# Expert weights split inside the attention loop, and token blocks of two halves taken in turn

## The chip, the cores and the metric

The kernel runs on one core of one Trainium2 chip. The metric is the device time of the whole launch in microseconds (us); lower is better. Engines are TensorE (PE in the profile), VectorE (DVE), ScalarE (ACT), GpSimd (POOL) and SyncE (SP). SyncE computes nothing here: its queue only issues transfers.

## The reference, cut to what matters

N is 4096 rows, D is 512 columns, there are 8 experts and each row takes 2 of them.

```python
q = layernorm(x) @ Wq.T + bq;  k = key @ Wk.T + bk;  v = value @ Wv.T + bv
s = (q @ k.T) / 64 * adj
s = where(abs(s) < 1e-5, -1e9, s)
x = x + softmax(s) @ v @ Wm.T + bm
z = layernorm(x)
gate = softmax(z @ Wg + bg)                     # 8 experts, the 2 largest kept and normalised
x = x + sum over the 2 experts of gate_e * (z @ We[e].T + be[e])
```

## The kernel before, in words

**Precision.** Every large matrix is held as two float16 halves, a high one and a low one (the rest after the high one is taken off), and a product is three matrix multiplications (high by high, high by low, low by high). ScalarE makes the high half, VectorE the low one.

**First stage.** Weights are folded, keys and values laid in two SBUF regions (`key_region`, `val_region`), queries sent to DRAM (`q_scratch`). The change doesn't touch it.

**Attention loop.** 32 tiles of 128 rows (T is 32), each in 8 chunks of 512 columns (C is 8). In iteration t TensorE computes the scores of tile t (`scores`) and the product of tile t-1's probabilities with the values (`times_values`), which runs two chunks late: chunks 6 and 7 of tile t-2 fall into the start of iteration t. One iteration on TensorE is in order: scores 0, scores 1, values 6 of t-2, scores 2, values 7 of t-2, scores 3, values 0 of t-1, scores 4, and so on. `times_values` of chunk 0 waits for `x1_done`, because the one PSUM bank of the output (`o_bank`) must have been read by `residual` of tile t-2 on VectorE (L1009). VectorE's iteration (`attend`, L1142) is in order: `low_half` of the probabilities of t-1 (L989), `times_adj` (L967), `mask` (L974, L977), after chunk 2 `residual` and the layer norm of tile t-2, later its routing (`route_top2`, `route_gates`, `route_slots`), at the end `softmax_bias` (L983, L985). ScalarE's (L757): two exponentials for each chunk of t-1 (L745, L750), each `absolute` of t (L737), the high half of the normalised row (`split_rows`) and one small exponential of the gates. ScalarE's first exponential waits for `softmax_bias`. SyncE's queue issues the adjacency, the transposes of the probabilities (`turn_probs`, L474), the transposed rows (`turn_rows`, L480), and at the end of the iteration the next query tile (L503).

**Routing.** GpSimd scatters each row, with its number and gate, into a DRAM table `slots[h]`, one for each half of the 4096 rows (`scatter_row`, L630); each expert has a region in it. After a half, `tables` (L1091) makes on VectorE the list of that half's 39 blocks of 128 slots with their experts, and `pad_regions` (L505) fills the ends of the regions from SyncE's queue: 8 transfers, each behind a load of a register from SBUF. `tables` uses some words of the buffer `q1_words`.

**The last tile.** Tile 31 has no scores beside it. The weights' buffers lie over the loop's, so here the code is written out: ScalarE's exponentials alternate with `expert_hi` and VectorE's `low_half` with `expert_lo`, which split the 8 experts' float32 weights into halves, 16 pieces of 128x1024, of which 8 come here and 8 in the first steps of the next stage. The weights come by 8 transfers of 1 MB into two buffers and the biases by one of 2 MB. `scatter_rows` of GpSimd waits for its transfers before it goes on to `inverse_deviation` of the next tile.

**Expert stage.** 78 blocks (39 of each half, half 0 first). For each: SyncE loads 128 rows (`load_block`, a ring of 8 buffers), TensorE transposes them (`turn_block`, two blocks ahead, L1430), ScalarE and VectorE make the halves (`block_hi`, `block_lo`), TensorE multiplies by the expert (`multiply_block`, L1280 to L1282, 12 multiplications), VectorE adds the bias (L1240), ScalarE multiplies by the gate (L822), GpSimd adds the rows in DRAM by an indirect transfer (L662). An add that starts another expert waits until those before it have landed. The first 23 blocks (EARLY) are written out with the remaining pieces of weights and the routing of tile 31 between them (its scatters after adds 10 and 13, its tables after block 9); the pads of half 1 are issued by SyncE before its block 23.

## Time and profile before

| | |
|---|---|
| median of 3 runs | 1904.72 us (1899.04 to 1904.8) |
| the profiled execution | 1899.79 us |
| its span, first to last instruction | 1898.1 us |
| TensorE busy | 1817.8 us, 96% of the span |
| VectorE, ScalarE, GpSimd busy | 62%, 38%, 13% |
| mean granted TensorE clock | 0.981 of full speed |

The profiled execution lies 1.7 us above its own span and 4.9 us below the median. A busy share is a mean over stages; the last sixth of the span looks otherwise than the loop, and the rows below are chosen by stage.

### The profile page before, as it was taken

How to read it: one execution, taken by the hardware profiler on the slowest of the kernel's cores; microseconds unless marked ns; L12 is line 12 of the kernel's file. 1: busy time of each engine (PE TensorE's matmuls, PEld its weight loads, DVE VectorE, ACT ScalarE, POOL GpSimd, SP SyncE). 2: the span in 40 equal slices, each digit the busy share in tenths (PEclk: the TensorE clock that was granted, in tenths of full speed). 3: DMA queues.
4: the chain of work that ended last, by engine and by line, in shares of the span. 5: the costliest groups of instructions: out<-in, count | busy, mean ns of one | idle time of the engine just before them, and what ended most of it. 6: DMA issues, size and time to landing. Idle time of an engine off the chain costs nothing.

```text
span 1898.1 us, 32739 instructions
## 1 busy us (share of the span) xinstructions
PE 1817.8 (96%) x8730; PEld 851.0 (45%) x8731; DVE 1176.2 (62%) x3056; ACT 730.1 (38%) x1381; POOL 239.4 (13%) x277
## 2 busy tenths in 40 slices
PE   8999999999999999999999999999999996789994
PEld 4544444444444444444444444444444443345552
DVE  2788766666666666666666666666666664634542
ACT  1444444443333344433333344433333442433341
POOL 1000000100000000000000000000000010444454
PEclk9999999999999999999999999999999998899997
DMA  5355455555555555555556555555555558788785
GB/s 200 111 177 188 172 136 124 140 142 137 139 138 133 133 133 145 137 142 134 139 128 176 135 135 144 134 145 133 138 133 136 134 137 244 180 194 165 162 161 78
DMA packets 410860, 279.67 MB, mean 147 GB/s; under 512 B 316737, under 2 KB 316737, under 8 KB 410690
## 3 DMA queue, kind: packets, MB, share of 16 engines
q1 hardware_dynamic: 390914, 234.55, 47.8%
q0 software_dynamic: 16736, 38.35, 10.2%
q10 hardware_dynamic: 3168, 6.29, 1.0%
q8 instruction: 16, 0.26, 0.1%
q14 instruction: 26, 0.21, 0.0%
HBM read 144.29 MB, written 59.33 MB: 107 GB/s over the span
## 4 chain that ended last, share of the span: by engine, by line
PE 75%; DVE 8%; DMA 7%; issue 5%; SPq 2%; ACT 2%; DVEq 0%; POOLq 0%; POOL 0%; ACTq 0%
PE ps L1280 16%; PE ps L1282 16%; PE ps L1281 16%; PE ps L1380 8%; PE ps L1381 8%; PE ps L1382 8%; DMA work<-q_scratch 4%; DVE work L967 2%; PE ps L1289 2%; PE ps L1430 1%; ACT work L737 1%; DMA work<-in_WeT 1%; DMA work<-work 1%; PE ps L1327 1%; DVE work L974 1%
## 5 line engine op out<-in xcount | busy, mean ns | idle before, releaser
L1280 PE MATMUL ps<-key_region,work 128*128 128x512 f16 (+1 forms) x1336 | 509.9, 382 | 9.8 <-DMA work<-q_scratch 7.0
L1281 PE MATMUL ps<-key_region,work 128*128 128x512 f16 (+1 forms) x1336 | 509.4, 381 | 0.0
L1282 PE MATMUL ps<-key_region,work 128*128 128x512 f16 (+1 forms) x1336 | 509.2, 381 | 0.0
L1380 PE MATMUL ps<-val_region,work 128*128 128x512 f16 x1024 | 389.6, 380 | 16.3 <-DMA work<-work 11.4
L737 ACT ACTIVATE work<-work 128x512 f32<-128x512 f32 x256 | 161.3, 630 | 597.2 <-DVE work L967 597.1
L1382 PE MATMUL ps<-val_region,work 128*128 128x512 f16 x1024 | 389.6, 380 | 0.0
L1381 PE MATMUL ps<-val_region,work 128*128 128x512 f16 x1024 | 389.5, 380 | 0.0
L967 DVE SCALAR_TENSOR_TENSOR work<-ps,r_cur,work 128x512 f32<-128x512 f32 x256 | 191.8, 749 | 179.0 <-PE ps L1282 163.3
L989 DVE TENSOR_TENSOR work<-work 128x512 f16<-128x512 f32 x256 | 176.4, 689 | 84.0 <-ACT work L750 83.1
L977 DVE CUSTOM_DVE_ANT_0 work<-work 128x512 f32<-128x512 f32 x256 | 177.3, 693 | 51.2 <-DVE work L974 51.0
L1280 PEld LDWEIGHTS ps<-key_region,work 128*128 128x128 f16 x1336 | 131.2, 98 | 172.9 <-issue 28.8
L745 ACT ACTIVATE work<-work,exp_bias 128x512 f32<-128x512 f32 x256 | 181.4, 708 | 65.6 <-DVE exp_bias L985 61.5
L1282 PEld LDWEIGHTS ps<-key_region,work 128*128 128x128 f16 x1336 | 131.4, 98 | 158.8 <-issue 3.4
L1281 PEld LDWEIGHTS ps<-key_region,work 128*128 128x128 f16 x1336 | 131.3, 98 | 148.0 <-issue 3.0
L750 ACT ACTIVATE work<-work,exp_bias 128x512 f16<-128x512 f32 x256 | 180.7, 706 | 0.0
L974 DVE TENSOR_SCALAR work<-work 128x512 f32<-128x512 f32 x256 | 109.2, 426 | 113.2 <-ACT work L737 109.2
L1380 PEld LDWEIGHTS ps<-val_region,work 128*128 128x128 f16 x1024 | 100.2, 98 | 131.8 <-DMA work<-work 12.0
L1382 PEld LDWEIGHTS ps<-val_region,work 128*128 128x128 f16 x1024 | 100.4, 98 | 122.0 <-issue 1.9
L1381 PEld LDWEIGHTS ps<-val_region,work 128*128 128x128 f16 x1024 | 100.4, 98 | 114.0 <-issue 1.5
L662 POOL DMA_INDIRECT out<-val_region,tok_ids x78 | 123.9, 1588 | 152.7 <-DMA out<-val_region,tok_ids 66.6
L627 POOL COPY work<-gate 128x1 f32<-128x1 f32 x64 | 14.6, 228 | 856.9 <-DVE slots_u L1089 776.6
L822 ACT ACTIVATE val_region<-work,tok_gates 128x512 f32<-128x512 f32 x78 | 56.3, 722 | 160.6 <-DVE work L1240 138.8
(149 smaller groups left out, 1542.9 us busy)
## 6 DMA issues: line engine op xcount, KB each, us to landing
work<-in_adj SPq DMA_DIRECT2D x256, 256.0 KB, 2.8
work<-slots SPq DMA_DIRECT2D x40, 257.0 KB
val_region<-slots SPq DMA_DIRECT2D x38, 257.0 KB
work<-in_valueT SPq DMA_DIRECT2D x8, 1024.0 KB, 6.8
work<-in_x SPq DMA_DIRECT2D x8, 1024.0 KB, 5.0
work<-in_keyT SPq DMA_DIRECT2D x8, 1024.0 KB, 5.4
q_scratch<-work SPq DMA_DIRECT2D x8, 1024.0 KB, 5.0
work<-q_scratch SPq DMA_DIRECT2D x32, 256.0 KB, 3.0
```

Of the source, the lines that this page charges most:

```text
L737: nc.scalar.activation(w[:, c * CW:(c + 1) * CW], s_adj[:, c % 2, :], ACT.Abs).then_inc(abs_done, 1)
L745: nc.scalar.activation(prob[:, c % 2, :], w[:, c * CW:(c + 1) * CW], ACT.Exp, bias=exp_bias[:, :], scale=1.0 / SS, accum_out=sum_part[:, c ...
L750: nc.scalar.activation(p_split[:, c, 0:CW], w[:, c * CW:(c + 1) * CW], ACT.Exp, bias=exp_bias[:, :], scale=1.0 / SS).then_inc(p_hi, 1)
L967: nc.vector.scalar_tensor_tensor(s_adj[:, c % 2, :], s_bank(c), r_cur[:, :], adj_in[:, c % ADJ, :], ALU.add, ALU.mult).then_inc(s_read, 1)
L977: nc.vector.tensor_tensor_reduce(out=masked, in0=s_adj[:, c % 2, :], in1=masked, scale=1.0, scalar=-3.0e38, op0=ALU.add, op1=ALU.max, accu ...
L989: nc.vector.tensor_tensor(p_split[:, c, CW:2 * CW], prob[:, c % 2, :], p_split[:, c, 0:CW], ALU.subtract).then_inc(p_lo, 1)
L1280: nc.tensor.matmul(bank, st[0], mv[0], start=(k == 0), stop=False)
L1281: nc.tensor.matmul(bank, st[0], mv[1], start=False, stop=False)
L1282: last = nc.tensor.matmul(bank, st[1], mv[0], start=False, stop=(k == n - 1))
L1380: nc.tensor.matmul(o_bank, st[0], mv[0], start=first, stop=False)
L1381: nc.tensor.matmul(o_bank, st[0], mv[1], start=False, stop=False)
L1382: last = nc.tensor.matmul(o_bank, st[1], mv[0], start=False, stop=final)
```

## The change

- Iterations 2 to 17 of the loop each take one half expert (256 of its 512 inputs). It is cut in 4 pieces of 128x256: ScalarE's queue loads a piece (`load_piece`), ScalarE makes the high half (`piece_high`), VectorE the low one (`piece_low`), and ScalarE's queue stores both to a DRAM tensor `we_halves` (`store_piece`). The buffers are in `q1_words`; so VectorE waits for all stores before `tables(0)`.
- In the last tile nothing is split. ScalarE's queue loads the finished halves, one expert at a time: experts 0 to 2 around the last exponentials, 3 to 7 in steps 0 to 4 of the expert stage, each with its own row of biases. SyncE tells TensorE by `we_ready` that an expert is there. The values product of tile 31 goes to another bank (`o_last`), so it doesn't wait for `residual` of tile 30.
- GpSimd no longer waits at the end of `scatter_rows`; it makes the deviations of tiles 30 and 31 before it scatters their rows, and tile 31's rows have a buffer of their own (`row_last`). `ranks` and `route_slots` of tile 30 move behind block 0 and 1, tile 31's routing comes at blocks 4 and 6, its scatters after adds 6 and 8.
- Blocks: 15 of half 0 (LEAD), then 48 in which half 0 and half 1 alternate, then 15 of half 1. The ring of row buffers has 16 places. The pads of half 1 are issued by ScalarE after block 9, and SyncE waits for them before its block 15.

The core of the diff:

```diff
-    EARLY = 23
-    LATE = 7
+    LEAD = 15
+    AHEAD = 2
+    TOKS = 16
...
 scalar
+            def load_piece(i, q):
+                nc.scalar.dma_start(we_stage, weT_parts[i, :, q // 2, q % 2, :]).then_inc(piece_loaded, 16)
+            def store_piece(i, q):
+                act.wait_ge(piece_lo, i * PIECES + q + 1)
+                settle()
+                nc.scalar.dma_start(we_dram[i, :, :, q * WP:(q + 1) * WP], we_halves).then_inc(piece_stored, 16)
+            def piece_high(i, q):
+                act.wait_ge(piece_loaded, i * (PIECES * 16) + (q + 1) * 16)
+                if not (is0(i) and q == 0):
+                    act.wait_ge(piece_stored, i * (PIECES * 16) + q * 16)
+                nc.scalar.activation(we_halves[:, 0, :], we_stage, ACT.Copy, scale=WS).then_inc(piece_hi, 1)
+            def attend(t, routes, splits=False):
+                if splits:
+                    load_piece(t - 2, 0)
                 for c in range(4):
                     exponent(t - 1, c)
                 absolute(t, 0)
+                if splits:
+                    piece_high(t - 2, 0)
                 exponent(t - 1, 4)
                 absolute(t, 1)
                 for c in range(5, C):
                     exponent(t - 1, c)
+                if splits:
+                    store_piece(t - 2, 0)
+                    load_piece(t - 2, 1)
...
                 absolute(t, 7)
+                if splits:
+                    piece_high(t - 2, 3)
+                    store_piece(t - 2, 3)
...
+            act.wait_ge(piece_stored, 16 * PIECES * 2 * E)
+            act.wait_ge(s_mm, T * C)
+            load_expert(0)
             for c in range(C):
                 exponent(T - 1, c)
-                if c >= 4:
-                    expert_hi(c - 4)
-                if c == 6:
-                    split_rows(T - 2)
+                if c == 3:
+                    load_expert(1)
+            act.wait_ge(p_hi, T * C)
+            load_bias(0)
+            load_bias(1)
+            split_rows(T - 2)
+            load_expert(2)
+            load_bias(2)
...
+                if st.first + 3 < E:
+                    load_expert(st.first + 3)
+                    load_bias(st.first + 3)
+                if st.first == 9:
+                    act.wait_ge(tables_done, 2)
+                    for e in range(E):
+                        at = act.value_load(pad_at[0:1, 1, e:e + 1], min_val=0, max_val=(DUMMY - 1) * P)
+                        nc.scalar.dma_start(slots[1][bass.ds(at, P), :], pad_row[:, :]).then_inc(padded[1], 16)
 vector
+            def piece_low(i, q):
+                dve.wait_ge(piece_hi, i * PIECES + q + 1)
+                nc.vector.scalar_tensor_tensor(we_halves[:, 1, :], we_stage, WS, we_halves[:, 0, :],
+                                               ALU.mult, ALU.subtract).then_inc(piece_lo, 1)
             def attend(t, h=None):
...
                 mask(t, 0)
+                if splits:
+                    piece_low(t - 2, 0)
                 times_adj(t, 1)
...
                 softmax_bias(t)
+                if splits:
+                    piece_low(t - 2, 3)
...
+            dve.wait_ge(piece_stored, 16 * PIECES * 2 * E)
             tables(0)
 sync
-            sp.dma_start(we_in[0], weT_v[0]).then_inc(we_loaded[0], 16)
-            for c in range(4):
+            for c in range(5):
                 turn_probs(T - 1, c)
+                if c == 3:
+                    residual_io(T - 2, 1)
             turn_rows(T - 2)
+            for c in range(5, C):
+                turn_probs(T - 1, c)
...
+            for e in range(2, E):
+                expert_ready(e)
+            sp.wait_ge(slotted, 32 * T)
+            sp.wait_ge(padded[1], 16 * E)
+            for st in turn_steps(0):
+                load_block(st)
 tensor
-                if c == 0 and not is0(t):
+                if c == 0 and isl(t, T):
+                    pe.wait_ge(s_read, T * C)
+                elif c == 0 and not is0(t):
                     pe.wait_ge(x1_done, t)
+                bank = o_last if isl(t, T) else o_bank
```

## Rows read from the trace of the kernel before

**Rows 1.** The page's first part: busy time, share and instructions by engine.
```profile
PE 1817.8 (96%) x8730; PEld 851.0 (45%) x8731; DVE 1176.2 (62%) x3056; ACT 730.1 (38%) x1381; POOL 239.4 (13%) x277
```
**Rows 2.** Windows, from:to, length, busy by engine, PE clock, DMA share, GB/s.
```profile
706.00:748.00 42.00, 41.77 (x203) 18.91 (x202) 26.95 (x75) 16.52 (x34) 3.04 (x5) 1.00 0.56 137
...
1560.60:1600.50 39.90, 26.65 (x116) 11.65 (x115) 19.84 (x50) 14.91 (x24) 3.23 (x5) 0.83 0.93 256
1600.50:1688.40 87.90, 73.55 (x347) 36.38 (x345) 48.91 (x141) 32.60 (x51) 36.43 (x26) 0.90 0.70 170
...
1697.40:1870.70 173.30, 173.30 (x904) 93.15 (x904) 83.58 (x221) 67.10 (x111) 80.16 (x52) 0.99 0.84 164
1870.70:1898.10 27.40, 0.03 (x1) 0.00 (x0) 0.69 (x1) 0.72 (x1) 9.25 (x6) 0.57 0.45 58
```
**Rows 3.** Timeline of TensorE after 1560 us: what began after its long gaps.
```profile
1562.78 0.38 PE L1380 MATMUL ps<-val_region,work 128*128 128x512 f16 x1 [1.82 <-DVE work L1009]
...
1576.27 0.39 PE L1380 MATMUL ps<-val_region,work 128*128 128x512 f16 x1 [2.97 <-DMA work<-work]
...
1589.05 0.61 PE L1380 MATMUL ps<-val_region,work 128*128 128x512 f16 x1 [8.46 <-DMA work<-work]
...
1617.08 1.09 PE L1430 MATMUL ps<-ident,val_region 128*128 128x128 f32 x4 [5.33 <-DVE work L1232]
...
1658.99 0.68 PE L1430 MATMUL ps<-ident,val_region 128*128 128x128 f32 x4 [2.83 <-DVE work L1232]
...
1697.40 1.11 PE L1430 MATMUL ps<-ident,val_region 128*128 128x128 f32 x4 [9.05 <-DMA val_region<-slots]
```
**Rows 4.** Timeline of TensorE, expert stage: transposes of two blocks, 14 blocks apart.
```profile
1711.03 0.60 PE L1430 MATMUL ps<-ident,work 128*128 128x128 f32 x4
...
1753.40 0.60 PE L1430 MATMUL ps<-ident,work 128*128 128x128 f32 x4
```
**Rows 5.** Timeline of one loop iteration: VectorE, ScalarE and TensorE around two hand-overs.
```profile
682.05 0.75 DVE L1009 SCALAR_TENSOR_TENSOR work<-ps,inv_sum,work 128x512 f32<-128x512 f32 x1
...
683.74 0.38 PE L1380 MATMUL ps<-val_region,work 128*128 128x512 f16 x1
...
680.15 0.63 ACT L737 ACTIVATE work<-work 128x512 f32<-128x512 f32 x1 [0.18 <-DVE work L967]
...
708.54 0.15 DVE L985 TENSOR_SCALAR exp_bias<-row_max 128x1 f32<-128x1 f32 x1
...
708.82 0.72 ACT L745 ACTIVATE work<-work,exp_bias 128x512 f32<-128x512 f32 x1 [1.88 <-DVE exp_bias L985]
```
**Rows 6.** Timeline of iteration 18, the one after tables(0): VectorE and TensorE.
```profile
980.82 0.75 DVE L1009 SCALAR_TENSOR_TENSOR work<-ps,inv_sum,work 128x512 f32<-128x512 f32 x1
...
981.71 0.38 PE L1380 MATMUL ps<-val_region,work 128*128 128x512 f16 x1 [3.04 <-DVE work L1009]
```
**Rows 7.** Timeline of ScalarE and VectorE: an issue of its queue, and pieces by length.
```profile
1617.57 0.38 ACTq L796 DMA_DIRECT2D work<-in_WeT  x1
1618.19 1.04 ACT L798 ACTIVATE key_region<-work 128x1024 f16<-128x1024 f32 x1
...
1621.13 0.68 DVE L1240 SCALAR_TENSOR_TENSOR work<-ps,work 128x512 f32<-128x512 f32 x1
1623.55 1.22 DVE L1197 SCALAR_TENSOR_TENSOR key_region<-work,key_region 128x1024 f16<-128x1024 f32 x1 [1.74 <-ACT key_region L798]
```
**Rows 8.** DMA issues: out<-in, queue, count, KB each, median us from issue to landing.
```profile
out<-work SPq DMA_DIRECT2D x32, 256.0 KB, 3.1
```
**Rows 9.** Timeline of SyncE's queue: pads of half 0, transposes of tile 31, pads of half 1.
```profile
1006.21 8.35 SPq L511 DMA_DIRECT2D slots<-pad_row  x8
...
1577.58 11.18 SPq L474 DMA_TRANSPOSE work<-work  x3
...
1681.56 11.26 SPq L511 DMA_DIRECT2D slots<-pad_row  x8
```
**Rows 10.** Timeline of VectorE: layer norm of tile 31, waiting for GpSimd.
```profile
1610.99 0.55 DVE L1032 TENSOR_SCALAR work<-work,moments,rstd 128x512 f32<-128x512 f32 x1 [6.20 <-POOL rstd L618]
```

More of the change, by code:

```diff
@@ L336, in graph_attention_moe_kernel @@
         padded = [sem(f"padded{h}") for h in range(HALVES)]
-        tok_loaded = [sem(f"tok_loaded{b}") for b in range(RING)]
+        tok_loaded = [sem(f"tok_loaded{b}") for b in range(TOKS)]
         tok_meta = sem("tok_meta")
@@ L371, in has, with ahead, lead_steps, turn_steps @@
             def has(self, back):
[L372 to L398 removed]
+                return self.later or self.first >= back
+            def ahead(self):
+                return Step(self.first + AHEAD, self.turn)
+        def lead_steps():
+            return [Step(s) for s in range(LEAD)]
+        def turn_steps(j, later=False):
+            return [Step(LEAD + i, j, later) for i in range(TURN)]
+        def tail_steps():
+            return [Step(s) for s in range(SEQ - LEAD, SEQ)]
+        TURNS = (SEQ - 2 * LEAD) // TURN
         block = ctx.enter_context(nc.Block())
@@ L626, in scatter_row @@
                 settle()
-                nc.gpsimd.tensor_copy(row_gate, gate[:, i:i + 1]).then_inc(gate_put, 1)
+                row = row_last if isl(t, T) else row_buf
+                nc.gpsimd.tensor_copy(row[:, D + 1:D + 2], gate[:, i:i + 1]).then_inc(gate_put, 1)
                 pool.wait_ge(gate_put, t * 2 + i + 1)
@@ L1168, in attend @@
                     route_low(t - 2, h)
+                if splits:
+                    piece_low(t - 2, 1)
                 mask(t, 4)
@@ L1172, in attend @@
                 times_adj(t, 6)
+                if splits:
+                    piece_low(t - 2, 2)
                 mask(t, 6)
@@ L1246, in _ @@
             route_stats(T - 1)
-            dve.wait_ge(be_loaded, 16)
             dve.wait_ge(tables_done, 1)
-            for i, st in enumerate(early_steps()):
-                if SPLIT_EARLY + i < 2 * E:
-                    expert_lo(SPLIT_EARLY + i)
-                block_lo(ahead(st))
-                if i == 0:
+            for st in lead:
+                block_lo(st.ahead())
+                if st.first == 0:
                     route_rows(T - 1)
                 block_bias(st)
-                if i == 0:
+                if st.first == 0:
                     route_low(T - 1, 1)
-                if i == 6:
+                if st.first == 4:
                     route_top2(T - 1)
                     route_gates(T - 1)
-                if i == 9:
+                if st.first == 1:
+                    route_slots(T - 2)
+                if st.first == 6:
                     route_slots(T - 1)
@@ L1264, in _ @@
             dve.wait_ge(tables_done, 2)
-            with dve.Fori(0, MIDDLE) as j:
-                for st in middle_steps(j):
-                    block_lo(ahead(st))
+            with dve.Fori(0, TURNS) as j:
+                for st in turn_steps(j):
+                    block_lo(st.ahead())
                     block_bias(st)
-            for st in end_steps():
+            for st in tail_steps():
                 if st.first + AHEAD < SEQ:
-                    block_lo(ahead(st))
+                    block_lo(st.ahead())
                 block_bias(st)
```

320 lines of the change are left out of this document (154 added, 166 removed).

## The prediction

> **What bounds the kernel now.** I read the page first: TensorE is busy for 96% of the span [rows 1], so time is won only where it is idle, or where its clock is low. The windows show where that is. An iteration of the loop keeps it busy 41.77 of 42 us [rows 2]; up to 1560.6 us little is to be had. After that there are three stretches. From 1560.6 to 1600.5 us (the values product of tile 31) it is busy 26.65 of 39.9 us at a mean clock of 0.83. From 1600.5 to 1688.4 us (the first blocks) 73.55 of 87.9 us at 0.90. From 1697.4 to 1870.7 us it never stops. The timeline names the gaps: two of 2.97 and 8.46 us behind transposes of probabilities, 5.33 us behind VectorE, 2.83 us behind VectorE while it makes the tables, 9.05 us behind a load of rows [rows 3]. What these stretches would take without gaps: the values product is 96 multiplications at 0.216 us (starts in a row on the timeline), 20.7 us, so 39.9 - 20.7 = 19.2 us are lost there. A block takes (1753.40 - 1711.03) / 14 = 3.03 us [rows 4], 78 of them 236.1 us; the stage takes 1870.7 - 1600.5 = 270.2 us, so 34.1 us are lost. The last 27.4 us [rows 2] are adds in DRAM after TensorE's end. Their number, and the half they belong to, stay as they are: 0.
>
> **What the change costs in the loop.** Each of iterations 2 to 17 gets 4 pieces on ScalarE and VectorE and 8 issues on ScalarE's queue. By busy time that is nothing: VectorE has 15 us to spare and ScalarE 25 in 42 [rows 2]. The question is where they stand in the chain, and two places matter.
>
> First, the iteration's end. ScalarE's first exponential now starts 0.28 us after `softmax_bias` starts [rows 5]. In the new order `piece_low` 3 comes behind `softmax_bias`, ScalarE waits for it, then issues the store, goes round the loop, issues the load of the next piece 0, and only then takes the exponential. A VectorE piece of 1024 columns takes 1.22 us and one of 512 0.68 us [rows 7]; the same line gives 0.41 us for 256. An issue takes 0.38 us [rows 7]. While a long ACTIVATE runs it is hidden (the ACTIVATE that follows this row starts as the earlier one ends), but here nothing runs. Sum: 0.41 + 2 x 0.38 + 0.3 for the semaphore, the registers and the branch (my choice between 0 and 0.8) = 1.5 us late.
>
> Second, inside it. `piece_low` 0 stands between `mask` 0 and `times_adj` 1, and the exponentials 5 to 7 hang on that: 0.4 us. A store and a load are issued between the last exponential and `absolute` 2 (680.15 us, [rows 5]): 0.76 us of issue, of which the running exponential hides all but some 0.2 us (between 0 and 0.5). `piece_low` 2 falls in a wait of VectorE for `absolute` 6, and pieces 1 and 3 of ScalarE in its waits: 0.
>
> So `residual` of the tile before comes 1.5 + 0.4 + 0.2 = 2.1 us later, and TensorE's values chunk 0 waits for it. What cover is there? `residual` starts at 682.05 us and TensorE takes that chunk at 683.74 us without a gap [rows 5]. In iteration 18 it did have to wait, and began 981.71 - 980.82 = 0.89 us after `residual` started [rows 6]. The cover is 683.74 - 682.05 - 0.89 = 0.8 us. TensorE would stand 2.1 - 0.8 = 1.3 us in each of the 15 iterations that have a piece 3 before them, and nothing gives it back, for everything behind it is paced by TensorE again. 15 x 1.3 = 19.5 us. Bounds: without the 0.3 and 0.2 it is 0.8 us, 12 us in all; with 0.8 and 0.5 it is 2.1 us, 31 us in all.
>
> Then `tables(0)`: VectorE now waits until the last store has landed. It is issued about 0.8 us after the bias and takes some 3.1 us to land, as a store to DRAM does [rows 8], where before `route_slots` ended 1 us after the bias. About 2.9 us go onto a gap that exists already, 3.04 us [rows 6], with no cover left. Loop: 19.5 + 2.9 = 22.4 us lost.
>
> The Trainium skill ("DMA: Bandwidth & Descriptors", section "Anatomy of one DMA — SWDGE (gpsimd) path") puts the dispatch of a transfer by the sequencer at about 50 ns. The row of this trace has 0.38 us for ScalarE's queue, so the row decides. By the page's figure two issues would cost 0.1 us in place of 0.76, the stall would be 0.65 us and the loop would lose about 13 us.
>
> **What it wins in the last tile.** The wait of 1.82 us for `residual` goes (another bank). Chunks 0 to 3 have their transposes early, chunk 4 follows. Chunk 5 now stands behind `turn_rows` of tile 30, whose row needs GpSimd, then ScalarE behind its last exponential: about 1570. With 1.25 MB of weights in flight its transpose lands at about 1578 us (before, three of them took 11.18 us to issue beside the weights and biases, [rows 9]), 5 us after TensorE wants it; the slower clock behind that costs some 3 us, the transposes of two blocks 1 us. Loss 9 in place of 19.2: 10 us won (6 to 14).
>
> **What it wins in the blocks.** Gone: the splitting of eight pieces beside the blocks, the wait of VectorE for GpSimd (6.20 us, [rows 10]) that led to TensorE's 5.33 us, and SyncE's pads ahead of the load that gave 9.05 us [rows 3]. Kept or new: the tables 2.8 us [rows 3]; the gates of tile 31 wait for tile 30's scatters, 1.5 us; block 6 is loaded behind `turn_rows`, beside 6 MB of weights, 1 us. The pads: SyncE's queue took 8.35 and 11.26 us for eight [rows 9]. ScalarE now does that with block 12 waiting behind it. Take 9.3 us. The cover is what the tables show: 5.5 us of VectorE cost TensorE 2.83 us [rows 3], so 2.7 us; 6.6 us are left. Then the pads must land before SyncE may load block 15: 2.5 us more. Slow clock 1.7 us. Sum: 2.8 + 1.5 + 1 + 6.6 + 2.5 + 1.7 = 16.1 in place of 34.1: 18 us won (9 to 23). Alternating the halves is 0: as many blocks, loads and starts of experts as before.
>
> **Sum.** -10 - 18 + 22.4 = -5.6 us. Against the profiled execution, 1899.79 us, that is 1894 us; against the median, which lies 4.9 us higher, 1899 us. I say 1898.
>
> **Rivals.**
> - *ScalarE's issues are hidden in the loop.* The queue might run ahead of the engine at the end too. For: it does so behind an ACTIVATE [rows 7]. Against: the store waits for VectorE, so it can't be early. Stall 0.65 us, loop 13 us: 1889 us. The skill's dispatch figure points the same way.
> - *The pads cost little.* If ScalarE's eight issues take 0.6 us each, or the ring of 16 rows covers them, 9 us less is lost: 1889 us.
> - *The loop loses more.* Late by 2.7 us in place of 2.1 (register work of the queue at the top): 15 x 1.9 + 2.9 = 31 us: 1908 us.
> - *The weights are in the way.* Five experts, 6.3 MB, are asked for in 15 us, while the stretch at 1560 us moved 256 GB/s at a share of 0.93 [rows 2]; that is 25 us of all the transfers. Rows, pads and scatters come late, and the tail wins only 14 us: 1912 us.
> - *The other side: TensorE's clock falls at each stall of the loop.* After 2.83 us of idle it ran low for a while (clock 0.90 in that stretch), after 3.04 us at iteration 18 it didn't. A fall costs 1.7 us a time (12 multiplications at twice 0.216). From 4 of 15 iterations on the gain is gone; with all 15, +25 us: 1923 us.
>
> **How the numbers follow.** The sum as forecast 0.36; issues hidden 0.17; cheap pads 0.12; loop loses more 0.10; weights in the way 0.15; clock 0.10. A measurement tells about 0.3%, 5.7 us, from no change. Faster: 0.17 + 0.12 + 0.16 of the forecast's own spread (1892 to 1905 us) = 0.45. Same: 0.20 + 0.10 = 0.30. Slower 0.25. The range leaves out the clock case and a little below: 1884 to 1917 us.
>
> **What would show it.** In the profile after: iterations 3 to 17 of 43.4 us in place of 42.1, each with a gap of 1.3 us on TensorE behind VectorE's `residual`, those from 19 on unchanged; a gap of about 6 us at iteration 18; the values product of tile 31 in about 30 us with one gap at chunk 5; a gap of about 6 us behind ScalarE's pads and then one behind the load of block 15. It is wrong if the loop's gap is absent (then faster by 20 us or more), or if the first 15 blocks lose over 25 us.

## The result, and the profile after

The changed kernel takes 1917.6 us (median of 5 runs, 1911.48 to 1919.96), the kernel before 1904.72 us beside it (5 runs, 1899.04 to 1907.65): a ratio of 1.007, 95% interval 1.0051 to 1.0088. It is slower, where I had forecast 1898 us. The span of the profiled execution grew from 1898.1 to 1913.1 us, by 15.0 us.

The page first: engines, the share of the chain by engine, and one group of instructions (busy time, mean ns of one, idle time just before them).

```profile
PE 1816.2 (95%) x8730; PEld 847.7 (44%) x8731; DVE 1181.4 (62%) x3104; ACT 736.7 (39%) x1429; POOL 244.5 (13%) x277
...
PE 55%; DVE 13%; DMA 12%; issue 9%; ACT 7%; SPq 2%; ACTq 1%; POOLq 1%; DVEq 1%; POOL 0%
...
L1444 PE MATMUL ps<-val_region,work 128*128 128x512 f16 x1024 | 389.9, 381 | 31.9 <-DVE work L1067 25.9
```

TensorE does the same work as before [rows 1]. The third row is the answer in small: the first multiplication of a values chunk waits 31.9 us in all, 25.9 of them for line 1067, which is `residual`. The windows put the rest in place; they are an iteration of the loop, the values product of tile 31, the first blocks, the blocks without gaps, and the adds behind the last product.

```profile
653.23:696.93 43.70, 42.02 (x202) 18.84 (x203) 28.42 (x79) 17.85 (x38) 3.28 (x5) 1.00 0.66 156
1588.67:1620.80 32.13, 25.19 (x113) 11.01 (x114) 10.26 (x34) 6.27 (x14) 2.22 (x3) 0.89 0.97 212
1620.80:1705.00 84.20, 64.33 (x323) 33.16 (x322) 38.87 (x132) 23.70 (x39) 31.97 (x26) 0.92 0.93 252
1705.00:1883.10 178.10, 177.76 (x932) 95.33 (x930) 87.15 (x230) 70.16 (x116) 85.42 (x55) 1.00 0.81 153
1883.10:1913.10 30.00, 0.00 (x0) 0.00 (x0) 0.69 (x1) 0.72 (x1) 9.32 (x6) 0.55 0.49 63
```

Beside [rows 2] that gives a ledger. Up to the values product of tile 31: 1588.67 against 1560.6 us, +28.1. The values product: 32.1 against 39.9, -7.8. All blocks: 262.3 against 270.1, -7.8. The adds behind them: 30.0 against 27.4, +2.6. Sum +15.1. (The loop began 1.5 us earlier in this execution, so it lost 29.6 us itself. The window of [rows 2] begins 0.36 us ahead of the gap in front of chunk 0, mine at that gap; from the same point the loop lost 29.2 us and the values product won 7.4.)

TensorE's timeline, what began after its gaps: the first row is one of the 15 iterations, the second iteration 18, then tile 31 and the blocks.

```profile
653.23 0.38 PE L1444 MATMUL ps<-val_region,work 128*128 128x512 f16 x1 [1.26 <-DVE work L1067]
...
1006.48 0.59 PE L1444 MATMUL ps<-val_region,work 128*128 128x512 f16 x1 [5.15 <-DVE work L1067]
...
1590.54 0.39 PE L1444 MATMUL ps<-val_region,work 128*128 128x512 f16 x1 [1.87 <-DMA work<-work]
...
1597.20 0.61 PE L1444 MATMUL ps<-val_region,work 128*128 128x512 f16 x1 [3.90 <-DMA work<-work]
...
1610.54 0.39 PE L1444 MATMUL ps<-val_region,work 128*128 128x512 f16 x1 [0.18 <-DMA work<-work]
...
1638.60 1.12 PE L1494 MATMUL ps<-ident,val_region 128*128 128x128 f32 x4 [4.58 <-DMA val_region<-slots]
...
1648.57 0.18 PE L1461 MATMUL ps<-picked,tri_half 128*128 128x8 f16 x1 [1.27 <-DVE picked L1139]
...
1678.14 1.09 PE L1494 MATMUL ps<-ident,val_region 128*128 128x128 f32 x4 [8.81 <-DVE work L1293]
...
1685.48 0.66 PE L1494 MATMUL ps<-ident,val_region 128*128 128x128 f32 x4 [2.61 <-DMA val_region<-slots]
```

And the hand-over at the end of an iteration, which answers to [rows 5]: the bias, the split of the last piece, the store, the load, the first exponential, and `residual`.

```profile
678.01 0.15 DVE L1043 TENSOR_SCALAR exp_bias<-row_max 128x1 f32<-128x1 f32 x1
678.11 0.43 DVE L1206 SCALAR_TENSOR_TENSOR work<-work 128x256 f16<-128x256 f32 x1
...
678.77 0.57 ACTq L775 DMA_DIRECT2D we_halves<-work  x1
...
679.83 0.35 ACTq L769 DMA_DIRECT2D work<-in_WeT  x1
...
680.31 0.72 ACT L751 ACTIVATE work<-work,exp_bias 128x512 f32<-128x512 f32 x1 [3.58 <-issue]
...
696.04 0.75 DVE L1067 SCALAR_TENSOR_TENSOR work<-ps,inv_sum,work 128x512 f32<-128x512 f32 x1
```

The reader is to see a chain in which each row waits for the one above. The exponential starts 2.30 us behind the bias, where it was 0.28 [rows 5]. `residual` comes 696.04 - 678.01 = 18.03 us behind the bias. In the kernel before, the bias of the iteration of [rows 5] stands at 666.38 us and `residual` at 682.05: 15.67.

### The profile page after: what moved, and what is told of

The parts are those of the page before. It is cut to its first block, busy times and chain, and to the rows that moved or that the text cites. A ratio compares the mean times of both kernels' runs of the same rounds, so it can differ in the third digit from the quotient of the medians.

```text
span 1913.1 us, 33565 instructions
## 1 busy us (share of the span) xinstructions
PE 1816.2 (95%) x8730; PEld 847.7 (44%) x8731; DVE 1181.4 (62%) x3104; ACT 736.7 (39%) x1429; POOL 244.5 (13%) x277
## 4 chain that ended last, share of the span: by engine, by line
PE 55%; DVE 13%; DMA 12%; issue 9%; ACT 7%; SPq 2%; ACTq 1%; POOLq 1%; DVEq 1%; POOL 0%
PE ps L1341 12%; PE ps L1343 11%; PE ps L1342 11%; DMA out<-val_region,tok_ids 6%; PE ps L1444 6%; PE ps L1445 6%; PE ps L1446 6%; DVE work L1025 4%; DMA work<-q_scratch 3%; ACT work L743 2%; ACT work L751 2%; DVE work L1032 2%; ACT work L756 2%; DMA slots<-work,slots_u 2%; PE ps L1350 1%
## 5 line engine op out<-in xcount | busy, mean ns | idle before, releaser
L1444 PE MATMUL ps<-val_region,work 128*128 128x512 f16 x1024 | 389.9, 381 | 31.9 <-DVE work L1067 25.9
L1293 DVE TENSOR_TENSOR work<-ps,work 128x512 f16<-128x512 f32 x78 | 53.9, 691 | 99.8 <-ACT work L866 99.8
```

Of the source, the lines that this page charges most:

```text
L1444: nc.tensor.matmul(bank, st[0], mv[0], start=first, stop=False)
```

## The experiments

Each kernel ran beside the kernel before on the same chip; ratios are to that. The kernel before took 1900.8 to 1904.7 us on these chips, so two kernels of different groups are better compared by their ratios (0.001 is 1.9 us) than by their times. They come in the order in which they ran. The first four asked one question of each part of the ledger.

### late_store: the pieces' issues among the exponentials

```diff
                 for c in range(4):
                     exponent(t - 1, c)
+                    if splits and c == 2:
+                        if not (isinstance(t, int) and t == 2):
+                            store_piece(t - 3, 3)
+                        load_piece(t - 2, 0)
...
                     piece_high(t - 2, 3)
-                    store_piece(t - 2, 3)
```
(With it the split of piece 0 goes behind the last exponential, and VectorE's half of it between `times_adj` 3 and `mask` 3.)

> The same 64 pieces, transfers and buffers as in the changed kernel; only their places differ: the store of piece 3 and the load of the next piece 0 are issued on ScalarE's queue under the exponential of chunk 3 of the next iteration, and piece 0 is split after the last exponential. Theory A (the late start of the exponentials and the piece before times_adj 1 delay residual, and TensorE waits for it): the gap of 1.2 to 1.6 us before the values chunk 0 is gone in iterations 3 to 17, an iteration is back at 42.1 us, and the time falls by 15 x 1.6 = 24 us, to 1893 to 1897 us. Rival B (the pieces' 1 MB of transfers and 2.5 us of ScalarE and VectorE work per iteration cost time wherever they stand): the iteration stays at 43.4 to 43.7 us and the time at 1913 to 1918 us. The gap after tables(0), about 5 us, stays in both.

Measured: 1890.92 us (5 runs), ratio 0.9948 (0.9931 to 0.9966). Windows of an iteration and of the values product of tile 31:

```profile
622.00:664.10 42.10, 41.86 (x204) 18.96 (x203) 28.41 (x79) 17.85 (x38) 2.96 (x5) 1.00 0.68 162
1565.20:1597.30 32.10, 23.99 (x112) 10.70 (x113) 10.27 (x34) 6.25 (x14) 2.19 (x3) 0.95 0.98 213
```

The gap is gone, `residual` is back at 15.69 us behind the bias, and an iteration at 42.1 us. The work in the loop is all still there (28.41 us of VectorE). From the bias of tile 31 to the end the trace has 330.6 us, the changed kernel 331.1, so the tail is the same. Theory A; the time is 2 us below its range. So the loop's loss is one of place, and the rest of the change is a gain.

### no_split: no pieces at all

```diff
-                splits = h == 0
+                splits = False
```
(The same on ScalarE. The experts' weights are loaded from other data of the same size, so this kernel's output is not the reference's.)

> Leaves the splitting out: no pieces in the loop, and the experts' halves are loaded at the same places, 1 MB each, from query tiles, so the expert products are of other numbers. It prices everything the split costs in the loop. Theory A: iterations of 42.1 us and the gap after tables(0) back at 3.0 us, so 27 to 28 us less than the changed kernel, 1889 to 1891 us. Rival B gives the same time here but differs in late_store. Rival C (the loss lies in the last stages): the time falls by less than 15 us.

Measured: 1882.34 us, ratio 0.9901 (0.9881 to 0.9921). From the bias of tile 0 to that of tile 31 the trace has 1298.6 us, late_store 1301.8, the changed kernel 1326.5, the kernel before 1297.4. Well placed, the pieces cost some 3 us in the loop, half of it at the tables, where the gap is 4.82 us in late_store and 3.26 here; badly placed, 28. The time itself is 7 us below the range of theory A, and 9.4 us below late_store by the two traces: 3.3 us in the loop, 1.9 behind the bias of tile 31, and 4.3 ahead of the bias of tile 0, where the two kernels are the same. That bias stands between 252.4 and 257.1 us over all the traces.

### pads_on_sync: the pads of half 1 back on SyncE

```diff
+            sp.wait_ge(tables_done, 2)
+            for e in range(E):
+                at = sp.value_load(pad_at[0:1, 1, e:e + 1], min_val=0, max_val=(DUMMY - 1) * P)
+                sp.dma_start(slots[1][bass.ds(at, P), :], pad_row[:, :]).then_inc(padded[1], 16)
```
(It stands ahead of block 15's load, and the lines on ScalarE are taken out.)

> Only the eight pads of half 1 go back from ScalarE's queue to SyncE's, ahead of its block 15. Theory A (ScalarE's queue is blocked for about 10 us by them, TensorE's gap of 8.8 us is that, and the 2.6 us behind it is the wait for pads and block 15): the gap of 8.8 us is gone, one of 3 to 5 us before block 15 stays, 6 to 9 us less: 1909 to 1912 us. Rival (the pads and the rows' load are the limit, whoever issues them): the gap moves to block 15 whole, and the time stays within 2 us of 1917.6.

Measured: 1914.2 us, ratio 1.0057 (1.0036 to 1.0078). TensorE's gaps, and the pads on SyncE's queue:

```profile
1636.59 0.38 PE L1455 MATMUL ps<-wg_split,work 128*128 128x16 f16 x8 [9.24 <-DMA work<-work]
...
1662.70 11.17 SPq L574 DMA_DIRECT2D slots<-pad_row  x8
...
1683.12 1.11 PE L1495 MATMUL ps<-ident,val_region 128*128 128x128 f32 x4 [5.31 <-DMA val_region<-slots]
```

The gap of 8.81 us goes, as said, but block 15 waits 5.31 us in place of 2.61, and block 6 4.82 in place of 4.58. A gap of 9.24 us for tile 31's transposed row stands ahead of all this; nothing in the edit stands ahead of it on any queue, and I take it for the spread of a transfer that travels beside the weights, without having shown it. From the bias of tile 31 to the end this trace has 332.5 us for 331.1, though the time is some 3 us less. The run decides little.

### weights_spread: experts 3 to 7 asked for at half the rate

```diff
-                if st.first + 3 < E:
-                    load_expert(st.first + 3)
-                    load_bias(st.first + 3)
+                if st.first in (0, 2, 4, 6, 8):
+                    load_expert(st.first // 2 + 3)
+                    load_bias(st.first // 2 + 3)
```

> Only the loads of experts 3 to 7 move, from steps 0, 1, 2, 3, 4 to steps 0, 2, 4, 6, 8. Theory A (6.3 MB at once hold up the rows of blocks 6 and 7 and the scatters): TensorE's gap of 4.6 us at 1638.6 shrinks to under 1.5 us, 3 to 5 us less, 1913 to 1915 us. Rival (SyncE's order, turn_rows of tile 31 ahead of those loads, makes the gap): it stays at 4 us or more and the time too; a wait for expert 7 before block 15 may even cost some us.

Measured: 1918.97 us, ratio 1.0086 (1.0062 to 1.011). TensorE's gaps:

```profile
1634.60 0.66 PE L1494 MATMUL ps<-ident,val_region 128*128 128x128 f32 x4 [0.50 <-DMA val_region<-slots]
...
1649.15 0.19 PE L1461 MATMUL ps<-picked,tri_half 128*128 128x8 f16 x1 [6.57 <-DVE picked L1139]
...
1680.06 1.09 PE L1494 MATMUL ps<-ident,val_region 128*128 128x128 f32 x4 [8.20 <-DVE work L1293]
1690.11 0.84 PE L1494 MATMUL ps<-ident,val_region 128*128 128x128 f32 x4 [4.75 <-DMA val_region<-slots]
```

The load of block 6 is no longer late (0.50 for 4.58), but the gates of tile 31 now are, and block 15 waits longer. From the bias of tile 31 to the end it takes 336.1 us, where the changed kernel takes 331.1. The same bytes come in, only later. The gap went as in theory A and the time did not; the rival had a later block 15 as a possibility. Whether bytes are the matter at all was still open.

### few_weights: an eighth of the bytes of six experts

```diff
+                    n = 2 * KC * D // 2 if e < 2 else 256
-                    nc.scalar.dma_start(we[:, e, a].rearrange("p h k o -> p (h k o)"),
...
+                    nc.scalar.dma_start(we[:, e, a].rearrange("p h k o -> p (h k o)")[:, 0:n],
...
```
(The source is cut to the same columns. The products of experts 2 to 7 use what else is in the buffer, so the output is not the reference's.)

> The changed kernel, but the loads of the split weights of experts 2 to 7 bring only an eighth of their columns (the products of those experts use what is left in the buffer, so the output is not the reference's); every issue, wait and semaphore stays. Theory A (the weights stand in the way of the small transfers at the end of attention and in the first blocks): the gaps behind transfers (3.90 us in tile 31, 4.58 us before block 7, 1.27 us before the ranks, 2.61 us before block 15) fall to a third or less, and the stretch from tile 31's bias to the end, 331.3 us in the changed kernel, gets 6 to 10 us shorter. Rival B (those gaps come from the order of the waits on the queue, and another row is late if one is not): the stretch keeps 331 within 2 us. Both: the gap of 8.81 us behind ScalarE's pads and the gaps of the loop (1.3 to 1.6 us an iteration) stay.

Measured: 1908.95 us, ratio 1.0041 (1.0024 to 1.0059). TensorE's gaps in the blocks:

```profile
1633.44 0.66 PE L1495 MATMUL ps<-ident,val_region 128*128 128x128 f32 x4 [2.11 <-DMA val_region<-slots]
...
1674.25 1.09 PE L1495 MATMUL ps<-ident,val_region 128*128 128x128 f32 x4 [7.71 <-DVE work L1294]
...
1680.80 0.66 PE L1495 MATMUL ps<-ident,val_region 128*128 128x128 f32 x4 [1.01 <-DMA val_region<-slots]
```

From the bias of tile 31 (1582.3) to the end (1906.1) it is 323.8 us, 7.3 less. The gap before block 6 halves, that before block 15 falls from 2.61 to 1.01, and the adds at the end take 2.2 us less. The gaps did not all fall to a third: the ranks wait 2.20 us in place of 1.27, and tile 31's chunks still wait 2.33 and 2.68. Ahead of TensorE's end it is 295.9 us in place of 301.1, where four other kernels with these blocks and pads and all the bytes (late_store, no_split, store_behind_first, issues_alone) have 299.3 to 301.6: the bytes cost some 5 us there. The 2.2 us of the adds (27.8 us) are not shown to be theirs, since two kernels with all the bytes, two_pads and late_two_pads, have 28.3 and 28.0. In sum it is what theory A had, gap by gap it is not.

### two_pads: the burst of eight taken apart

```diff
-                if st.first == 9:
-                    act.wait_ge(tables_done, 2)
-                    for e in range(E):
+                if 9 <= st.first < 13:
+                    if st.first == 9:
+                        act.wait_ge(tables_done, 2)
+                    for e in range(2 * (st.first - 9), 2 * (st.first - 9) + 2):
```

> The changed kernel, with the eight pads of half 1 on ScalarE's queue issued two at a time, behind the gates of blocks 9, 10, 11 and 12, in place of eight behind block 9's. Theory A (the stall of 8.81 us is the burst of issues: 9.71 us for eight, 1.2 us each, while TensorE has one block in hand): two take 2.4 us a block, under the 3.03 us of a block less ScalarE's own 1.5 to 2 us, so the stall shrinks to under 3 us in all, the stretch from tile 31's bias to the end gets 5 to 8 us shorter and the time 1910 to 1913 us. Rival B (the pads have to land before block 15's load, and they land later when they are spread): the stall moves to block 15, whose gap grows from 2.61 us to 6 or more, and the time stays within 2 us of the changed kernel's.

Measured: 1920.77 us, ratio 1.0113 (1.0088 to 1.0137), slower than the changed kernel (1.007, 1.0051 to 1.0088), by 8 us if the ratios are compared; by the traces the stretch from the bias of tile 31 to the end is 5.7 us longer. In the changed kernel the burst and ScalarE's next row are:

```profile
1666.86 9.71 ACTq L895 DMA_DIRECT2D slots<-pad_row  x8
1676.67 0.60 ACT L866 ACTIVATE work<-ps 128x512 f16<-128x512 f32 x1 [10.00 <-issue]
```

In this one, ScalarE's queue, SyncE's load of block 15, and TensorE's transpose of it are:

```profile
1665.55 1.88 ACTq L896 DMA_DIRECT2D slots<-pad_row  x2
...
1682.05 1.45 ACTq L896 DMA_DIRECT2D slots<-pad_row  x2
...
1687.00 0.34 SPq L541 DMA_DIRECT2D val_region<-slots  x1
...
1689.93 1.11 PE L1495 MATMUL ps<-ident,val_region 128*128 128x128 f32 x4 [15.01 <-DMA val_region<-slots]
```

The stall behind the burst is gone (what is left of it is 1.03 us). But the last pair is issued at 1682 us instead of before 1676.6, and SyncE, which waits for it to land, issues the load of block 15 at 1687.0: 15.01 us of idle where two gaps had 11.4 together. Rival B, and more than it had. The pads stand between two limits, and the second is there only because block 15 is a row of half 1.

### in_order: half 0's blocks, then half 1's

```diff
-                middle = LEAD <= first < SEQ - LEAD
-                self.h = (first - LEAD) % 2 if middle else int(first >= LEAD)
...
+                self.h = int(first >= BLOCKS)
+                self.at = first if is0(turn) else first + turn * TURN
```
(SyncE and GpSimd take the 48 middle blocks one by one in place of a loop; SyncE waits for the pads ahead of block 39.)

> The changed kernel, with the blocks in the order half 0 then half 1 in place of alternating from block 15 on; pads, scatters and weights stay where they are, and SyncE waits for them before block 39. Theory A (alternating costs by what block 15 has to wait for, and by adds that wait for each other at both halves' ends): the gap of 2.61 us before block 15 goes, the drain of the adds behind the last product falls from 30.1 to 27.6 us as in the kernel before, and the time is 3 to 5 us below the changed kernel's. Rival B (block 15's wait is hidden and the drain is what the last two adds cost in either order): within 1.5 us. Both: the gap of 8.81 us behind the pads' issues stays.

Measured: 1910.4 us, ratio 1.0048 (1.0031 to 1.0065). That is 7 us below the changed kernel's time, but on another chip, where the kernel before was 4 us faster too; the ratios lie 4 us apart and their intervals overlap, the two profiled spans 5.9. TensorE's gap behind the pads, and the window from TensorE's end on:

```profile
1679.45 1.09 PE L1488 MATMUL ps<-ident,val_region 128*128 128x128 f32 x4 [6.12 <-DVE work L1287]
```
```profile
1881.60:1907.20 25.60, 0.00 (x0) 0.00 (x0) 0.69 (x1) 0.72 (x1) 9.32 (x6) 0.58 0.47 61
```

Block 15's gap is gone, and the adds end 25.6 us behind TensorE in place of 30.0. From the bias of tile 31 to TensorE's end it wins 1.5 us only: its two gaps here are 5.3 us shorter together, but from 1620.8 to 1705 us its granted clock is 0.88, in the changed kernel 0.92. So most of the difference is at the end, more than I had expected. Theory A, for the gap; for the end it is argued, since the loop of GpSimd was undone with the order. Over all traces the adds take 27.8 to 30.9 us behind TensorE with alternating halves (10 kernels) and 25.6 to 27.3 with halves in order (3 kernels).

### late_two_pads: both repairs, halves alternating

The diffs of late_store and two_pads together.

> The changed kernel with both repairs: in the loop the store of a tile's last piece and the load of the next are issued among the next tile's exponentials (as in late_store, which took 1890.9 us), and the pads of half 1 are issued two at a time behind blocks 9 to 12. Theory A: the two gains add, 1883 to 1887 us. Rival B (the pads' stall moves to block 15): 1889 to 1892 us.

Measured: 1893.79 us (10 runs), ratio 0.9959 (0.9944 to 0.9973). The gap before block 15 is 16.92 us. Rival B again, 2 us above its range: spreading the pads wins nothing here, and may lose 2 us (by the ratios) or more (the stretch from the bias of tile 31 to the end is 337.4 us for late_store's 330.6).

### store_behind_first: the wait moved by one chunk

```diff
                 for c in range(4):
                     exponent(t - 1, c)
+                    if splits and c == 0:
+                        if not (isinstance(t, int) and t == 2):
+                            store_piece(t - 3, 3)
+                        load_piece(t - 2, 0)
```
(The store at the iteration's end and the load at its top go. VectorE's order stays as in the changed kernel.)

> The changed kernel, with the store of a tile's last piece and the load of the next piece issued behind the first exponential chunk of the next tile instead of ahead of it; VectorE's order is not touched. In the changed kernel the first exponential starts 2.0 us later than in the kernel before, of which some 1.1 us are the wait for the split of the last piece (0.43 us and its hand-overs) and 0.9 us the two issues (0.57 and 0.35). Theory A (only the wait is taken away by this; the issues still delay chunks 1 to 7, and VectorE's rows follow those): the gap ahead of the values product falls from 1.3 to 1.6 us to 0.4 to 0.8, the loop's 15 tiles get 11 to 16 us shorter, 1902 to 1907 us. Rival B (behind chunk 0 the issues are covered as they are behind chunk 2 in late_store): the gap goes, the loop gets 22 to 27 us shorter, 1891 to 1895 us. Rival C (the wait is all on the issues' side, which stay ahead of chunks 1 to 7): the gap stays over 1 us and the time over 1910.

Measured: 1888.86 us, ratio 0.9927 (0.9911 to 0.9942). The hand-over again:

```profile
664.29 0.15 DVE L1046 TENSOR_SCALAR exp_bias<-row_max 128x1 f32<-128x1 f32 x1
...
664.57 0.72 ACT L751 ACTIVATE work<-work,exp_bias 128x512 f32<-128x512 f32 x1 [1.57 <-DVE exp_bias L1046]
...
665.06 0.57 ACTq L775 DMA_DIRECT2D we_halves<-work  x1
...
665.79 0.50 ACTq L769 DMA_DIRECT2D work<-in_WeT  x1
...
666.34 0.72 ACT L751 ACTIVATE work<-work,exp_bias 128x512 f32<-128x512 f32 x1 [0.35 <-issue]
```

One chunk of exponentials covers nearly all of it. VectorE's split ends at 664.81 us, and the store's issue begins 0.25 us behind it, as in the changed kernel; but it now runs under the exponentials of chunk 0, and ScalarE is idle 0.35 us in place of 2. `residual` comes 680.75 - 664.29 = 16.46 us behind the bias, 0.79 later than in the kernel before; that is the cover which the prediction had found, and TensorE has no gap. Rival B; the time is 2 us below its range.

### order_two_pads: pads that nobody waits for

The diffs of in_order and two_pads together.

> The changed kernel with its blocks in the order half 0 then half 1 (in_order took 1910.4 us), and the pads of half 1 issued two at a time behind blocks 9 to 12 on ScalarE's queue (with alternating blocks that took 1920.8 us, since block 15 then waited 15.0 us). Theory A (the pads hurt by one of two ways: issued in a burst they stall ScalarE, spread they come too late for block 15, which is a row of half 1 only because the halves alternate): here nothing needs the pads before block 39, the gap of 6.12 us behind the burst falls to under 1.5 us and no other comes: 1903 to 1907 us. Rival B (another wait is next in line behind the same burst, such as the adds of the first blocks): 1908 us or more.

Measured: 1905.56 us (11 runs), ratio 1.0024 (1.0015 to 1.0033). What is left of the pads' stall:

```profile
1673.55 0.63 PE L1489 MATMUL ps<-ident,val_region 128*128 128x128 f32 x4 [1.03 <-DVE work L1288]
```

From the pads on no gap is longer than 1.1 us, where in_order has 6.12. (Block 6 still waits 4.38 us, ahead of them.) By the ratios the edit loses 8 us with alternating halves and wins 5 with halves in order; by the traces, from the bias of tile 31 to the end, it loses 5.7 and wins 4.2. Theory A.

### late_order_two_pads: the three repairs

The diffs of late_store, in_order and two_pads together.

> The three repairs together: store and load of the pieces among the exponentials, blocks in the order half 0 then half 1, pads of half 1 two at a time behind blocks 9 to 12. Of the change it keeps the splitting in the loop, the loading one expert at a time, the order of the last tile and the rings of 16. Theory A (the repairs are independent and add): late_store's 1890.9 us less 7 for the order and less 4 to 6 for the pads, 1878 to 1882 us, 20 us or more below the kernel before. Rival B (they share one cover): 1884 to 1888 us.

Measured: 1881.06 us (4 runs), ratio 0.9884 (0.9869 to 0.9899): the fastest kernel of the study. Its windows over the values product of tile 31 and the first blocks:

```profile
1564.00:1596.50 32.50, 26.00 (x114) 10.94 (x113) 10.31 (x34) 7.00 (x16) 1.74 (x3) 0.89 0.98 220
1596.50:1680.70 84.20, 69.98 (x353) 35.95 (x352) 40.64 (x138) 25.59 (x42) 32.82 (x27) 0.94 0.96 276
```

Its ratio is 12 us below late_store's, where theory A had 11 to 13. By the traces the tail wins 6.8 us on top of late_store and 10.1 on top of the changed kernel, so the repairs add up within some 3 us. In the same 84.2 us TensorE is busy 5.7 us more than in the changed kernel.

### issues_alone: the issue without the wait

```diff
-                if splits:
-                    load_piece(t - 2, 0)
+                if splits and not (isinstance(t, int) and t == 2):
...
+                    for n in range(2):
+                        nc.scalar.dma_start(extra[n], weT_parts[0, :, 0, 0, 0:8]).then_inc(extra_done, 16)
                 for c in range(4):
                     exponent(t - 1, c)
...
```
(The rest is store_behind_first; the extra loads go from one DRAM tensor to another and nobody reads them.)

> store_behind_first (1888.9 us; residual 16.46 us after the bias, no gap ahead of the values product) with two more issues on ScalarE's queue ahead of the first exponential of each iteration from the third on: two loads of 128x8 elements into scratch rows that nobody reads, which wait for nothing that is late. They stand where the changed kernel has its store and its load, without the wait for VectorE's split. Theory A (an issue costs ScalarE its 0.35 to 0.57 us wherever it stands, as the term of 2 x 0.38 in the forecast has it): residual 17.2 to 17.5 us after the bias, a gap of 0.7 to 1.0 us in 14 iterations, 1899 to 1903 us. Rival B (ScalarE waits 1.9 us for the bias anyway, so issues that wait for nothing are done by then, and the changed kernel's loss comes from the wait that holds them behind the bias): residual stays at 16.5 us, no gap, within 2 us of 1888.9.

Measured: 1889.99 us, ratio 0.9924 (0.9898 to 0.995). The two extra issues, the bias, the first exponential, and `residual`:

```profile
663.83 1.24 ACTq L791 DMA_DIRECT2D extra<-in_WeT  x2
...
665.47 0.15 DVE L1054 TENSOR_SCALAR exp_bias<-row_max 128x1 f32<-128x1 f32 x1
...
665.75 0.72 ACT L753 ACTIVATE work<-work,exp_bias 128x512 f32<-128x512 f32 x1 [1.57 <-DMA extra<-in_WeT]
...
681.99 0.74 DVE L1078 SCALAR_TENSOR_TENSOR work<-ps,inv_sum,work 128x512 f32<-128x512 f32 x1
```

Two issues ahead of the exponentials take 1.24 us of the queue and cost nothing: they end 0.4 us before the bias, in ScalarE's own wait, and `residual` is 16.52 us behind it. (The releaser printed in the third row is the last transfer that landed; the row it waits for is the bias.) Rival B.

## Why the prediction was wrong, point by point

The forecast was a sum of -10, -18 and +22.4 us. Each term had its sign right, each was mis-sized, and all in the same direction, so the sum came out slower and not faster: -7.8, -7.8, +29.6, and +2.6 where I had 0 (less the 1.5 us by which this execution began its loop earlier: +15.1).

**The loop.** The mechanism was right: the chain from `piece_low` 3 over the store to the first exponential, the cover of 0.8 us, one gap behind `residual` in 15 iterations, cadence of all others unchanged. The term "1.5 us late" measured 2.02, and "2.1 later" for `residual` measured 2.36. So the delays inside the iteration, forecast at 0.4 + 0.2, came to 0.34, and those at its end were the ones mis-sized. With the cover of 0.8 that is 1.6 us an iteration ((959.16 - 347.29) / 14 = 43.705 us against 42.1), 24.1 us for fifteen, in place of 19.5. Two parts were mis-sized. The two issues, 2 x 0.38, took 0.57 + 0.35 = 0.92 us. The steps between, 0.3 in the forecast, took more: the store's issue starts 0.23 us behind the end of the split, the load's 0.49 us behind the end of the store's, and the exponential 0.13 us behind that. The rival "the loop loses more" had 1.9 us an iteration and missed by as much on the other side; its total of 31 us lay nearer than 22.4, because the tables cost more than either had.

The Trainium skill ("DMA: Bandwidth & Descriptors", section "Anatomy of one DMA — SWDGE (gpsimd) path") has some 50 ns for a dispatch; by that the loop would have lost 13 us. The section is about transfers that GpSimd issues, and the rows here, 0.57 and 0.35 us, are of ScalarE's queue: they do not refute the figure, they show that it is not the price of an issue here.

issues_alone sharpens what the step says. The issues as such are free at this place, since ScalarE waits for the bias anyhow. They cost because the first of them waits for VectorE's split of a piece that is made behind the bias. The rival "issues are hidden" was right of issues and wrong of these. store_behind_first shows that the same issues with the same wait are covered one chunk later.

**The tables.** The gap at iteration 18 grew from 3.04 to 5.15 us, by 2.1 where I had 2.9. But I had no term for the clock. These are the windows from the gap's end on, in the kernel after, and the window around that gap in the kernel before:

```profile
1006.40:1016.00 9.60, 9.52 (x32) 3.86 (x33) 4.58 (x13) 1.71 (x3) 0.57 (x1) 0.71 0.54 125
1016.00:1026.00 10.00, 10.00 (x55) 4.61 (x54) 4.86 (x11) 0.99 (x3) 0.00 (x0) 1.00 0.59 131
```
```profile
960.00:1040.00 80.00, 76.01 (x367) 34.29 (x366) 53.39 (x153) 31.68 (x65) 6.48 (x10) 1.00 0.65 164
```

Behind 5.15 us of idle TensorE ran at a granted clock of 0.71 over 9.6 us, partly at the lower of its two levels (1.2 GHz of 2.4): 2.8 us lost. Behind 3.04 us it stayed at 1.00. So the tables cost 2.1 + 2.8 = 4.9 us in place of 2.9 (from bias to bias, over the three iterations from the tables on, 134.5 us against 130.0: 4.5). The length of the gap does not set the price alone: over the same 9.6 us the clock was 0.84 in weights_spread behind 5.16 us, and 0.82 in no_split behind 3.26 us. The rival that had the clock fall at each stall of the loop was wrong: after gaps of 1.2 to 1.6 us the iterations' windows show 1.00. Its price also had a slip: 12 x 0.216 is 2.6 us and not 1.7. In the kernel before, the clock was 0.83 in the 10 us behind the gap of 2.83 us, which is 1.7 us.

**The last tile.** "The wait of 1.82 us for `residual` goes" failed: the bank is free, but the transposed probabilities of chunk 0 land just as late, and the gap is 1.87 us. "Chunks 0 to 3 have their transposes early" failed too: chunk 1 waits 3.90. And the gap that I had put at chunk 5, 5 us, is 0.18. The sum was nearly right: 32.1 us for "about 30", 7.8 us won and not 10, within the range of 6 to 14. That the places were wrong and the sum nearly right is luck. The clock's share, 3 us, was right: in the 10 us behind the gap of 3.90 us it was 0.73, so 2.7 us were lost.

**The blocks.** This is the largest error, 10 us. Block time without gaps is 236.1 us, so the stage of 262.3 us loses 26.2 us where I had listed 16.1 and had said that over 25 us would prove me wrong. Item by item, predicted against measured: block 6's load behind `turn_rows` 1 against 4.58; gates of tile 31 1.5 against 1.27; pads' issues 6.6 against 8.81, as the burst took 9.71 us and I had credited it with 2.7 us of cover where it had 0.9; pads' landing 2.5 against 2.61; tables 2.8 against 1.1 at most; the clock 1.7 against 3.9. The load was mis-sized most, then the clock and the pads. These add up to 22.3 us; the other 4 are in smaller waits for which the forecast had no term. Two windows behind the two long gaps:

```profile
1638.60:1648.60 10.00, 8.73 (x33) 4.07 (x34) 3.96 (x18) 2.01 (x4) 5.90 (x5) 0.75 1.06 367
1678.14:1690.00 11.86, 8.96 (x39) 4.54 (x40) 5.28 (x14) 3.73 (x6) 6.23 (x4) 0.88 0.84 179
```

0.25 x 10 + 0.12 x 11.86 = 3.9 us, where I had one fall of 1.7. few_weights shows that some 5 us before TensorE's end are the weights' bytes in the way of rows. The rival "weights in the way", to which I gave 0.15, had the tail's gain at 14 us, and it measured 15.6, or 13.0 with the adds; its cause is less than half of the 12.4 us that are missing from my 28, so its number is partly luck. The rest is the pads, the clock and the places of tile 31's waits.

**Alternating the halves, 0.** This was wrong. It makes block 15 the deadline for the pads of half 1, as in_order and two_pads show. And the adds end later with it: 30.0 against 27.4 us, and 25.6 in in_order. The argument "as many blocks, loads and starts of experts as before" counted work and not order. What makes the end later was not isolated: GpSimd's waits for adds to land come at other places in the two orders, in_order also undoes GpSimd's loop, and with one and the same order it varies from 27.8 to 30.9 us.

**The sum.** Two rivals were half true at once (the loop loses more, the weights are in the way), and I had priced each as if the other parts went as forecast. The one was to add 10 us to the forecast, the other 14; both together would be 1922 us, and the result, 1917.6, lies between the forecast and that, just above the range's end of 1917.

## What to carry to other kernels

A transfer that waits for another engine is issued at the place where its wait ends, with a running instruction over it; one chunk of exponentials was enough, and made 27 us of difference. Two issues at a place where ScalarE waits anyhow cost nothing (issues_alone). Pads, resets and other rows that are needed "by then" have two prices, the stall of the engine that issues them and the deadline of who reads them: an order that brings the reader forward takes away the room to spread them. And when two unfavourable cases have different causes, their sum belongs in the range.

## What the runs showed of the hardware

- An issue on ScalarE's queue took 0.35 to 0.61 us for the load of a piece and 0.57 to 0.68 us for the store. Eight pads in a burst took 9.71 us, two at a time (two_pads) 1.38 to 1.88. Divided, that is 1.21 us each against 0.7 to 0.9, but the row of eight holds seven steps from one issue to the next, each with its load of a register, and the row of two only one. The issue of the first pad by itself is 0.38 us, so a step is (9.71 - 0.38) / 7 = 1.33 us in the burst and 1.00 to 1.50 in the pairs (an estimate from these rows). So a pad is no dearer in a burst; what differs is how long the engine's next instruction stands behind them.
- The clock: gaps of 1.2 to 1.6 us in the loop left it at 1.00, one of 3.04 us too. One of 5.15 us brought it to 0.71 over the following 9.6 us, one of 5.16 us (weights_spread) to 0.84, one of 3.26 us (no_split) to 0.82.
- An eighth of the weights' bytes (in six of the eight experts) made the stretch from tile 31's bias to TensorE's end 5.2 us shorter and the gap of one row's load fall from 4.58 to 2.11 us, with every issue in its place: transfers in the way, not issues, made over half of that gap.
